# Another order of the work inside a slot of a software pipeline over four engines

## What is computed

```
xn = layernorm(x)
s  = recurrence(xn)                 # u = gelu(.)*sigmoid(.), then s_t = s_{t-1} A^T + u_t B, y = s C^T + D
g  = silu(transformer(xn))          # 6 layers
out = x + s * g

each of the 6 layers:
  q, k, v = split(shift_tokens(x) @ Wqkv)       # 16 heads of 64
  q, k = rotary(l2norm(q) * qs), rotary(l2norm(k) * ks)
  x = softmax(window mask(q k^T * 8)) v @ Wo + x      # windows of 32 tokens, looking one window back
  xn = layernorm(shift_tokens(x)) * g + b
  a, gate = split(xn @ W1 + b1)
  x = a * gelu(gate) @ W2 + b2 + x
```

## Time and profile before

| | us |
|---|---|
| median of 3 runs | 1901.24 (1900.99 to 1901.6) |
| the profiled execution | 1909.64 |
| its span (first to last instruction) | 1907.8 |
| TensorE busy | 1716.4 (90%) |
| VectorE busy | 1468.1 (77%) |
| ScalarE busy | 1095.4 (57%) |
| GpSimd busy | 1088.4 (57%) |
| granted TensorE clock | 0.984 of full |

### The profile page before, as it was taken

How to read it: one execution, slowest core, us unless ns; L and a number is a source line. 1 busy time by engine, 2 the same in 40 slices (tenths; PEclk the granted TensorE clock), 3 DMA queues, 4 the chain that set the end, 5 groups by cost and what they waited for, 6 DMA issues and landing times.

```text
span 1907.8 us, 75895 instructions
## 1 busy us (share of the span) xinstructions
PE 1716.4 (90%) x30558; PEld 1209.9 (63%) x30558; DVE 1468.1 (77%) x2727; ACT 1095.4 (57%) x2035; POOL 1088.4 (57%) x970
## 2 busy tenths in 40 slices
PE   5689999999989999999999998999998999999986
PEld 2356666666666666666666666666666666666664
DVE  4688787878877877877887887777887888787764
ACT  2255665656655565656656665656665566566653
POOL 0366665556656655655666666565655655665540
PEclk9699999999999999999999999999999999999999
DMA  2122223222222322222322222222222232222222
GB/s 97 29 78 63 55 57 77 64 66 71 58 48 72 77 69 49 69 57 57 78 63 67 65 62 55 77 64 69 66 55 55 67 77 65 71 58 56 53 54 67
DMA packets 82897, 122.09 MB, mean 64 GB/s; under 512 B 25168, under 2 KB 28752, under 8 KB 82256
## 3 DMA queue, kind: packets, MB, share of 16 engines
q1 hardware_dynamic: 82512, 116.84, 24.4%
HBM read 20.28 MB, written 2.10 MB: 12 GB/s over the span
## 4 chain that ended last, share of the span: by engine, by line
PE 57%; ACT 15%; issue 15%; DVE 11%; ACTq 1%; DMA 0%; DVEq 0%; SPq 0%
PE QKb L450 12%; PE F L573 10%; PE O L510 9%; PE S L498 6%; PE VTb L473 5%; PE S L450 4%; ACT L665 3%; ACT E L665 3%; PE F L596 3%; ACT v_tok L676 3%; PE F L597 2%; PE S L521 2%; PE S L491 2%; ACT KT L659 2%; DVE hid L904 2%
## 5 line engine op out<-in xcount | busy, mean ns | idle before, releaser
L975 POOL TENSOR_TENSOR t<-t 128x512 f32<-128x512 f32 x384 | 488.2, 1271 | 426.1 <-DVE t L835 425.8
L835 DVE TENSOR_TENSOR t<-QKb,table 128x1024 f32<-128x1024 f32 x384 | 469.2, 1222 | 285.0 <-ACT sq L650 281.1
L969 POOL TENSOR_TENSOR t<-t,rn 128x512 f32<-128x512 f32 x384 | 413.7, 1077 | 178.0 <-DVE rn L896 170.9
L450 PE MATMUL QKb<-wq_sb,x_sh 128*128 128x512 f32 x768 | 413.3, 620 | 60.9 <-DVE t L835 51.8
L650 ACT ACTIVATE sq<-QKb 128x512 f32<-128x512 f32 x384 | 229.1, 597 | 332.9 <-PE QKb L450 332.8
L473 PEld LDWEIGHTS VTb<-cst,t 128*128 128x128 f32 x1536 | 193.7, 142 | 204.1 <-issue 202.3
L960 POOL TENSOR_TENSOR E<-E,rs 128x512 f32<-128x512 f32 x192 | 200.2, 1043 | 159.9 <-DVE rs L868 159.9
L510 PE MATMUL O<-PT,V 64*64 64x32 f32 x12288 | 232.2, 221 | 39.6 <-issue 38.1
L682 ACT COPY OT<-O 128x512 f32<-128x512 f32 x192 | 112.5, 586 | 263.8 <-PE O L510 263.8
L510 PEld LDWEIGHTS O<-PT,V 64*64 64x64 f32 x12288 | 205.9, 135 | 62.4 <-issue 43.7
L473 PE MATMUL VTb<-cst,t 128*128 128x128 f32 x1536 | 232.6, 274 | 0.3 <-issue 0.3
(11 more groups left out here) (136 smaller groups left out, 2197.5 us busy)
## 6 DMA issues: line engine op xcount, KB each, us to landing
V<-v_tok SPq DMA_DIRECT2D x1440, 64.0 KB, 2.0
wq_sb<-in_wqkv SPq DMA_DIRECT2D x36, 256.0 KB, 3.1
wo_sb<-in_wo SPq DMA_DIRECT2D x6, 512.0 KB, 3.6
w_sb<-in_w SPq DMA_DIRECT2D x6, 341.0 KB
w_sb<-in_w SPq DMA_DIRECT2D x6, 192.0 KB
y_spill<-OT SPq DMA_DIRECT2D x1, 1024.0 KB, 4.8
V<-y_spill SPq DMA_DIRECT2D x1, 1024.0 KB, 8.0
out<-V SPq DMA_DIRECT2D x4, 256.0 KB, 2.9
```

What stands on the lines that cost most here:

```text
L450: return pe.matmul(out_, x_sh[:, pr, P * tile:P * (tile + 1)], wq_sb[:, col:col + 512], start=True, stop=True)
L835: dve.tensor_tensor(t12[:, v, :, :].rearrange("p c (h d) -> p c h d", h=8), QK_ps.rearrange("p (h d) -> p h d", h=8).unsqueeze(1) .to_broa ...
L969: pool.tensor_tensor(w, w, rn[:, vv // 4, 8 * (vv % 4):8 * (vv % 4 + 1)].unsqueeze(2) .to_broadcast([P, 8, DH]), ALU.mult).then_inc(qk_nor ...
L975: pool.tensor_tensor(w, w, t12[:, v, 1, :].rearrange("p (h c d) -> p h c d", h=8, c=2)[:, :, ::-1, :], ALU.add).then_inc(add_done, 1)
```

## The change

The stages are the same, each on its engine; only their places in the lists change.

- W1 chunks 0 and 1 move from slot 7 to slot 0 of the next step (`F_W1` 31 to 32), to the end of the slot's list on TensorE. The Gelu stays in slot 0.
- TensorE: in odd slots the waits for the product with V (`pt_evac`, `o_evac`, `v_moved`) come ahead of the transposes L473 instead of behind them. The mean comes behind W1 chunk 2; BC comes behind Wo.
- ScalarE: the feed-forward square (L646, slot 2) comes behind the attention's square and transposed copy instead of ahead of them. The other moved blocks (OT copy, `xs` copies) share no slot with what they pass.
- VectorE: `newton` moves from the end of its slots (1 and 5) to their beginning; centring comes ahead of `hidden` 2; `finish` moves to the end of slot 3; the sum of squares L844 comes ahead of L835 instead of behind it.
- GpSimd: the scaling L969 comes ahead of the normalising L960.

```diff
-F_BC, F_XN, F_W1, F_GEL, F_HID, F_W2, F_END = 30, 31, 31, 32, 33, 34, 35
+F_BC, F_XN, F_W1, F_GEL, F_HID, F_W2, F_END = 30, 31, 32, 32, 33, 34, 35
...
@@ TensorE, step @@
                         project(QK_ps, par, tile, QK_COLS[2 * half + kind]).then_inc(qk_ready, 1)
+                    a, k, st, pr = quad(s, par, v, L_PV)
+                    if live(a, QUADS):
+                        if k == 0:
+                            for c in range(4):
+                                wait(pe, v_moved[c], moved(st + 1, c))
+                        wait(pe, pt_evac, a + 1)
+                        wait(pe, o_evac, a)
                     u, vv, st, pr = unit(s, par, v, L_TR)
...
-                    f, pr = batch(s, par, v, F_MEAN)
...
-                    f, pr = batch(s, par, v, F_BC)
...
                     for k in range(QPS):
                         f, pr = batch(s, par, v, F_WO + k)
...
+                    f, pr = batch(s, par, v, F_BC)
...
+                    f, pr = batch(s, par, v, F_HID)
+                    if f is not None:
+                        ff_w1(f, pr, [2])
+                    f, pr = batch(s, par, v, F_MEAN)
...
                     f, pr = batch(s, par, v, F_W1)
...
-                    f, pr = batch(s, par, v, F_HID)
-                    if f is not None:
-                        ff_w1(f, pr, [2])
@@ ScalarE, step @@
-                    f, pr = batch(s, par, v, F_SQ)
-                    if f is not None:
-                        wait(act, cent_done, f + 1)
-                        act.activation(xq[:, :], xc[:, :], ACT.Square).then_inc(xq_done, 1)
                     if live(g, UNITS):
...
+                    f, pr = batch(s, par, v, F_SQ)
+                    if f is not None:
+                        wait(act, cent_done, f + 1)
+                        act.activation(xq[:, :], xc[:, :], ACT.Square).then_inc(xq_done, 1)
@@ VectorE, step @@
+                    u, vv, st, pr = unit(s, par, v, L_NEWTON)
+                    f, _ = batch(s, par, v, F_NEWTON)
+                    if vv % 4 == 0 and (live(u, UNITS) or f is not None):
+                        newton(st, vv // 4, u, f)
                     recurrence(in_fill(s, v, 0))
+                    f, pr = batch(s, par, v, F_CENT)
...
+                    u, vv, st, pr = unit(s, par, v, L_SS)
+                    if live(u, UNITS) and vv % 2 == 0:
+                        wait(dve, sq_done, u + 2)
+                        dve.tensor_reduce(ss[:, vv // 4, 8 * (vv % 4):8 * (vv % 4) + 16],
...
                     recurrence(in_fill(s, v, 1))
-
-                    u, vv, st, pr = unit(s, par, v, L_NEWTON)
-                    f, _ = batch(s, par, v, F_NEWTON)
-                    if vv % 4 == 0 and (live(u, UNITS) or f is not None):
-                        newton(st, vv // 4, u, f)
+                    f, pr = batch(s, par, v, F_END)
+                    if f is not None:
+                        finish(f, pr)
```

More of the change, by code:

```diff
@@ L576, in step @@
                                 mm.then_inc(wo_ready, 1)
+                    f, pr = batch(s, par, v, F_BC)
+                    if f is not None:
+                        wait(pe, diag_done, f + 1)
+                        wait(pe, ff_final, f)
+                        pe.matmul(BANK_BC[:, 0:N], ones[:, :], diag[:, :, :].rearrange("p t q -> p (t q)"),
+                                  start=True, stop=True).then_inc(bc_ready, 1)
+                    f, pr = batch(s, par, v, F_HID)
[3 more added lines that the diff above has]
+                    if f is not None:
+                        wait(pe, xs_done, 2 * (f + 1))
+                        wait(pe, hid_done, (f - 1) * NCH + 2)
+                        pe.matmul(BANK_MEAN[:, 0:N], mean_w[:, :], xs[:, :], start=True, stop=True)\
+                          .then_inc(mean_ready, 1)
                     f, pr = batch(s, par, v, F_W1)
@@ L660, in step @@
                                  VT_ps.rearrange("p (i q) -> p i q", i=4)).then_inc(tr_evac, 1)
+                    f, pr = batch(s, par, v, F_SQ)
+                    if f is not None:
+                        wait(act, cent_done, f + 1)
+                        act.activation(xq[:, :], xc[:, :], ACT.Square).then_inc(xq_done, 1)
+                    a, k, st, pr = quad(s, par, v, L_PV)
+                    if live(a, QUADS):
+                        wait(act, o_ready, a + 1)
+                        if isinstance(a, int) and a == QPS:
+                            wait(act, y_saved, 16)
+                        act.copy(OT[:, pr, 2 * k:2 * k + 2, :], O2[:, :, 0:N]).then_inc(o_evac, 1)
                     a, k, st, pr = quad(s, par, v, L_EXP)
@@ L665, in step @@
                         act.activation(E[:, k, :], E[:, k, :], ACT.Exp).then_inc(exp_done, 1)
+                    f, pr = batch(s, par, v, F_MID)
+                    if f is not None:
+                        wait(act, mid_done, f + 1)
+                        act.copy(xs[0:64, :], xm[0:64, pr, :]).then_inc(xs_done, 1)
+                        act.copy(xs[64:P, 1:N], xm[64:P, pr, 0:N - 1]).then_inc(xs_done, 1)
                     a, k, st, pr = quad(s, par, v, L_PT)
@@ L676, in step @@
                         act.copy(v_tok[:, c // 2, 512 * (c % 2):512 * (c % 2 + 1)], V_ps).then_inc(v_evac, 1)
[L677 to L687, removed]
                     if v == 5 and live(s + 1, STEPS):
@@ L782, in step @@
                     g = s * SLOTS + v
+                    u, vv, st, pr = unit(s, par, v, L_NEWTON)
+                    f, _ = batch(s, par, v, F_NEWTON)
+                    if vv % 4 == 0 and (live(u, UNITS) or f is not None):
+                        newton(st, vv // 4, u, f)
                     recurrence(in_fill(s, v, 0))
+                    f, pr = batch(s, par, v, F_CENT)
+                    if f is not None:
+                        wait(dve, mean_ready, f + 1)
+                        dve.tensor_tensor(xc[:, :], xs[:, :], BANK_MEAN[:, 0:N], ALU.subtract)\
+                           .then_inc(cent_done, 1)
                     f, pr = batch(s, par, v, F_HID)
@@ L808, in step @@
                            .then_inc(mid_done, 1)
[L809 to L813, removed]
                     f, pr = batch(s, par, v, F_XN)
@@ L970, in step @@
                                            .to_broadcast([P, 8, DH]), ALU.mult).then_inc(qk_norm, 1)
+                    a, k, st, pr = quad(s, par, v, L_NORM)
+                    if live(a, QUADS):
+                        wait(pool, rs_done, a + 1)
+                        w = E[:, k, :].rearrange("p (c k) -> p c k", k=KEYS)
+                        pool.tensor_tensor(w, w, rs[:, k, :].unsqueeze(2).to_broadcast([P, 8, KEYS]),
+                                           ALU.mult).then_inc(p_norm, 1)
                     if live(g, UNITS):
```

27 lines of the change are left out of this document (3 added, 24 removed).

## The result

The changed kernel takes 1910.77 us (median of 7 runs) against 1901.24 us before in the same comparison: ratio 1.0043, 95% interval 1.0028 to 1.0057. It is slower by 0.4%, and I had forecast 1792. The profiled execution spans 1909.5 us.

A forecast was written before the change was run, and what follows sets the result against it. TensorE was near the bound, stopped by VectorE's order. Stops of 2.97 us less 0.35 for newton gave 2.62 a step, 118 us over 45 steps, less 8.5 for holes: 1792 us, range 1760 to 1850.

The forecast's parts named there:

- the four stops: TensorE waits in slots 0 to 3 (0.65, 0.65, 0.86, 0.65 us), all forecast to go; TensorE's own work 33.3 us a step.
- W1 to slot 0: W1 chunks stand where TensorE waited 0.65 us between slots 0 and 1; that stop goes, slot 7 loses nothing.
- square and centring: In slot 2, the new order removes the 0.65 us at slot 3's scores and the 0.86 to within 0.05.
- nothing waits for `t12` of slot 7: Slot 7 without W1: `t12` ends at 14.8 us, TensorE asks for the bank at 15.2 to 15.4, so no stop.
- Sum of squares "cost nothing": Even slots: the 1.14 us sum ahead of `t12` fits VectorE's idle time (2.18 and 3.12 us in slots 0 and 4).
- Newton's 0.35 a step: Newton at the head of slots 1 and 5: L884 and L887 wait for GpSimd, delaying TensorE 0.35 us a step.
- my upper bound: Upper limit of newton's delay, about 1.3 us a step: each newton waits for another GpSimd scaling, less the slack.
- third rival: Newton's six two-input operations on VectorE also wait for GpSimd, until normalising ends: 1.85 us a step, about 1875 us; chance 0.05.
- second rival: Holes grow when TensorE no longer pauses, 1.94 instead of 1.2 us a step: about 1820 us; chance 0.12.
- Holes: TensorE gaps without a semaphore, 1.2 us a step on average; those waits had absorbed now show, costing 8.5 us.
- the thinnest place: Product-with-V waits ahead of the transposes: in slot 3 the probabilities' copy is ready at 29.6, wanted at 29.9; forecast cost nothing.
- the last rival: Nothing changes: VectorE returns exactly the stops that it gives up, 1901 us; chance 0.04.

The follow-up runs named there:

- the cut kernel: The changed kernel with each of GpSimd's three operations of a slot cut to 64 of its 512 columns: 1760.36 us, one run.

## Why the prediction was wrong

*The bound and the four stops: right.* TensorE's own 33.3 us a step is what the cut kernel ran at, and all four stops went away as described.

*W1 to slot 0, square and centring: right, the first too small.* Alone they are worth 52 and 59 us. I had priced the stops one by one, as if they were independent; the first one fed the second and most of the third. That nothing waits for `t12` of slot 7 was wrong with W1 moved alone (0.56 us).

*Sum of squares "cost nothing": wrong for slots 2 and 6.* I read the idle time ahead of `t12` in slots 0 and 4 and carried it to all even slots. Alone it costs 1.4%, or 0.50 us a step (36.76 against 36.26).

*Newton's 0.35 a step: the step that failed.* The mechanism was found (L884 and L887 each wait for one GpSimd operation), the term was mis-sized. From slot 4's projection L884 ends at 4.47 us and L887 at 5.47, as forecast (4.48 and 5.49). Newton ends at 7.62 and not at 6.8. The missing 0.8 is the first L891, 0.98 us long where I had counted the 0.19 of the like operations. I let it off because `diag`, also with two inputs in SBUF, had taken 0.42 in 48 cases. But in 45 of these cases `diag` had begun 0.04 to 0.05 us before GpSimd's operation, and in the other three nothing ran beside it. The row showed who waits when VectorE comes first, and I read it as who waits at all. Newton longer than 3 us was one of my own signs of being wrong, and it took 3.73.

*What the term measured.* Steps without a hole give it: 36.43 us with newton first and 34.59 with newton last, all else as changed, so newton's place costs 1.84 a step, over my upper bound of 1.3. In it is `diag`, which came second and took 1.30 where I had counted 0.42. The other 1.3 between 33.3 and 34.59 stands without newton. The sum of squares in slots 2 and 6 is 0.6 of it (34.0 without it); the other 0.7 was not taken apart. The three parts tried alone in the kernel before change its step by -1.08, -1.18 and +0.50, which gives 34.50 against these 34.59: they add up.

*The third rival had it.* The Trainium skill, "GPSIMD Engine Reference", section "Key points", names VectorE instructions in a two-port mode and those with two SBUF inputs. For the second kind the rows of the changed kernel agree (L891 0.98, `diag` 1.30). L884, L887 and L822 would have to be of the first kind; the rows show that they are held and not the mode. Taken at its word for two inputs it was my third rival, and I gave it 0.05. That rival's 1.85 a step is close to the 1.84 that newton's place measured, in part by luck, as it did not count `diag`. Its 1875 us was too low by 36, because it took the rest of my sum over, the free sum of squares above all. (In the second rival 0.74 x 45 is 33 us, so 1825 and not 1820.)

*Holes: not the cause.* Idle time of TensorE put down to "issue" was 53.0 us before and 50.1 after, ahead of L510 38.1 and 32.2. What grew is the part ahead of L450, most of it where the loop starts over, from 9.1 to 17.9 us, and the steps there, from 39.6 to 41.8 us before to 42.0 to 43.9. That part is 15.2 us with W1 alone moved and 17.0 with GpSimd's operations cut, so newton's waits do not make it; its cause stays open. The wait that I called the thinnest place held TensorE up ahead of the transposes by 0.4 us in the whole run.

*The outcome has the shape of the last rival*, "VectorE returns exactly the stops that it gives up", which I had listed without a mechanism. 2.97 us a step went and about 3.1 came. That the two are nearly equal is chance: with one wait added on GpSimd the same order gains 5.6%.

## What to carry to other kernels

A row shows the cost of an operation in its neighbourhood: before moving it, look at what will run beside it on the other engine, and who of the two starts first. When busy time grows without new instructions, compare the mean durations line by line, then lay the two engines' timelines side by side and look for ends that coincide. Small operations in a dependent chain belong where the engine that holds them up is idle; where they can't be moved, let the engine with time to spare wait for them. After an order has changed, price its parts again: a stop can hang on an earlier one.

## What the runs showed of the hardware

- A VectorE instruction that is caught ends only when GpSimd's current instruction has: 0.19 us of work (L891) became 0.98. Newton's small ones end 0.03 to 0.06 us behind it, L822 0.15 and `diag` 0.28. When GpSimd has three instructions in a row, the next ones are held one after another.
- Held here: `tensor_scalar` on SBUF (L884, L887, L822), and `scalar_tensor_tensor` and `tensor_tensor` with both inputs in SBUF (L891, `diag`). Not held in the changed kernel's run, with a GpSimd operation already running: the reduction L833 (144 times, 1.20 to 1.22 us, as alone), the reciprocal L869 (186 times, 0.20) and `t12`, which reads one input from PSUM (95 times, 1.21 to 1.23, as alone).
- The engine that comes second pays. `diag` that began first took 0.42 while GpSimd's scaling grew from 1.04 to 1.28. The changed kernel shows both cases: in 40 steps `diag` began 0.01 to 0.03 us behind the scaling, took 1.30 and left it at 1.04 (first pair); in 5 it began 0.06 to 0.07 ahead, took 0.41, and the scaling took 1.25 (second pair).

```profile
1036.13 1.04 POOL L962 TENSOR_TENSOR t<-t,rn 128x512 f32<-128x512 f32 x1
1036.15 1.30 DVE L804 TENSOR_TENSOR xq<-cst,rn 128x256 f32<-128x256 f32 x1
...
1790.18 0.41 DVE L804 TENSOR_TENSOR xq<-cst,rn 128x256 f32<-128x256 f32 x1
1790.25 1.25 POOL L962 TENSOR_TENSOR t<-t,rn 128x512 f32<-128x512 f32 x1
```
